# A graph network's attention passes: the sums in hand multiplied on ScalarE instead of VectorE

## The reference

```python
xl = (x @ Wl).reshape(n, H, C)
xr = (x @ Wr).reshape(n, H, C)
e = jax.nn.leaky_relu(xl[src] + xr[dst], NEG_SLOPE)
score = jnp.einsum('ehc,hc->eh', e, att)
smax = jax.ops.segment_max(score, dst, num_segments=n)
ex = jnp.exp(score - smax[dst])
denom = jax.ops.segment_sum(ex, dst, num_segments=n)
alpha = ex / jnp.maximum(denom[dst], 1e-16)
out = jax.ops.segment_sum(alpha[:, :, None] * xl[src], dst, num_segments=n)
```

## Time and profile before

| | us |
|---|---|
| median of 3 runs | 2442.35 |
| lowest, highest | 2435.42, 2443.87 |
| the profiled execution | 2437.04 |
| its span, first to last instruction | 2435.2 |

### The profile page before, as it was taken

One profiled execution on the slowest core, in us unless ns is written; L12 is line 12 of the kernel. 1 busy time (PEld: TensorE's weight loads), 2 busy tenths in 40 slices (PEclk: granted clock), 3 DMA queues, 4 the chain that ended last, 5 costly groups with the idle time before them and its releaser, 6 DMA issues. The chain is left out here.

```text
span 2435.2 us, 38029 instructions
## 1 busy us (share of the span) xinstructions
PE 1901.7 (78%) x8650; PEld 1361.5 (56%) x8650; DVE 1752.1 (72%) x3972; ACT 1347.5 (55%) x5197; POOL 1466.3 (60%) x1630
## 2 busy tenths in 40 slices
PE   4655566665569998689999999976789999999976
PEld 4443444444357775356666666653456666666654
DVE  8544333333346668589999999978489999999976
ACT  2255545555400004358777878744368788778733
POOL 3277777777700005777777677726777776767712
PEclk9777878778789999899999999998899999999987
DMA  3297676775668883355555555540355555555542
GB/s 105 65 193 173 172 163 170 177 168 167 145 206 267 269 266 112 94 158 158 154 149 166 149 151 152 147 99 30 89 158 157 158 154 151 150 154 151 142 106 83
DMA packets 225447, 370.18 MB, mean 152 GB/s; under 512 B 40453, under 2 KB 168711, under 8 KB 225256
## 3 DMA queue, kind: packets, MB, share of 16 engines
q1 hardware_dynamic: 157169, 192.55, 30.1%
q0 software_dynamic: 64512, 171.82, 25.8%
q10 hardware_dynamic: 3574, 3.66, 0.5%
HBM read 272.85 MB, written 101.50 MB: 154 GB/s over the span
## 5 line engine op out<-in xcount | busy, mean ns | idle before, releaser
L1166 POOL DMA_INDIRECT gath<-gather_table,SRCI x880 | 835.7, 950 | 321.3 <-issue 260.6
L1387 ACT ACTIVATE gath<-gath 128x32 f32<-128x32 f32 x3264 | 710.8, 306 | 0.0
L1218 PE MATMUL p_sums<-gath,OH 128*128 128x272 f32 x1760 | 474.2, 410 | 99.9 <-DVE gath L1113 60.9
L768 POOL DMA_INDIRECT rows_by_src<-gath,node x440 | 433.9, 986 | 139.6 <-issue 116.7
L702 PE MATMUL p_expd<-node,HOTS 128*128 x880 | 295.3, 496 | 228.9 <-DVE HOTS L661 220.8
L1218 PEld LDWEIGHTS p_sums<-gath,OH 128*128 128x128 f32 x1760 | 318.7, 193 | 213.9 <-issue 139.0
L702 PEld LDWEIGHTS p_expd<-node,HOTS 128*128 128x128 f32 x880 | 208.5, 248 | 304.7 <-issue 268.9
L1188 PE MATMUL p_expd<-node,LBC 128*128 x2640 | 328.9, 275 | 0.0
L1188 PEld LDWEIGHTS p_expd<-node,LBC 128*128 128x128 bf16 x2640 | 260.9, 99 | 60.3 <-issue 1.9
L1260 DVE TENSOR_REDUCE scores<-work 128x32 f32<-128x1056 f32 x220 | 274.6, 1248 | 5.7
L1182 PE MATMUL p_expd<-gath,ident 128*128 128x512 f32 x440 | 236.7, 620 | 42.8 <-DMA gath<-gather_table,SRCI 40.9
(11 more groups left out here) (291 smaller groups left out, 2767.3 us busy)
## 6 DMA issues: line engine op xcount, KB each, us to landing
gath<-rows_by_src SPq DMA_DIRECT2D x122, 514.0 KB
LBC<-hots_by_node SPq DMA_DIRECT2D x220, 128.0 KB
HOTS<-hots_by_edge SPq DMA_DIRECT2D x220, 128.0 KB, 2.6
LBC<-local_rows SPq DMA_DIRECT2D x110, 128.0 KB
hots_by_node<-gath SPq DMA_DIRECT2D x110, 128.0 KB, 5.7
hots_by_edge<-gath SPq DMA_DIRECT2D x110, 128.0 KB, 4.2
gath<-gather_table,SRCI POOLq DMA_INDIRECT x880, 3.0
rows_by_src<-gath,node POOLq DMA_INDIRECT x440, 4.9
```

What stands on the lines that cost most here:

```text
L768: pool.indirect_dma_start(sup_d[:, :], bass.IndirectOffsetOnAxis(POSI[:, i:i + 1], 0), U[:, q % 4, g, :], None, bounds_check=EP - 1, oob_i ...
L1166: pool.indirect_dma_start(ROWS[:, i % (RING * G), 0:XW], None, tab_d[:, :], bass.IndirectOffsetOnAxis(SRCI[:, i:i + 1], 0)).then_inc(gathe ...
L1218: ins = pe.matmul(sums[k][:, 0:RW], OH[:, a % 2, g, :], slots(a, g, g + 1)[:, 0, :], start=(g % 2 == 0), stop=(g % 2 == 1))
L1387: ins = act.activation(R[:, h * C:(h + 1) * C], R[:, h * C:(h + 1) * C], ACT.Copy, scale=R[:, D + h:D + h + 1])
```

## The change

ScalarE multiplies the 256 features of the sums in hand: a new function `regrow` does one operation for each head, with the head's factor as the scale. It stands behind the weighing of group 4u (`weigh_own`) and ahead of ScalarE's `ends` of the same step. VectorE keeps the 8 exponentials. A new semaphore, `regrown`, holds VectorE's next addition until the eight operations are done, and holds the next factor until the factor before it has been used.

```diff
@@ add_sum, VectorE
                             if a or k:
                                 dve.wait_ge(added, 2 * a + k)
+                            if a and a % WG == 0 and k == 0:
+                                dve.wait_ge(regrown, a // WG)
                             dve.tensor_tensor(ACC[:, bass.ds(j, 1), :], ACC[:, bass.ds(j, 1), :], sums[k][:, 0:RW].unsqueeze(1), ALU.add).then_inc(added, 1)
@@ grow, VectorE
-                            R = ACC[:, bass.ds(tile, 1), 0:D].rearrange("p a (h c) -> p (a h) c", h=H)
                             S = ACC[:, bass.ds(tile, 1), D:XW].rearrange("p a h -> p (a h)")
                             dve.wait_ge(grown, u + 1)
                             dve.wait_ge(added, 2 * WG * u)
-                            dve.tensor_tensor(R, R, GROW[:, :].unsqueeze(2).broadcast_to([P, H, C]), ALU.mult)
                             link(dve.tensor_tensor(S, S, GROW[:, :], ALU.mult))
@@ ScalarE
+                        def regrow(u):
+                            tile = tiles_of(act, 2 * WG * u, 1)[0]
+                            act.wait_ge(added, 2 * WG * u)
+                            act.wait_ge(grown, u + 1)
+                            for h in range(H):
+                                R = ACC[:, bass.ds(tile, 1), h * C:(h + 1) * C].rearrange("p a c -> p (a c)")
+                                ins = act.activation(R, R, ACT.Copy, scale=GROW[:, h:h + 1])
+                            ins.then_inc(regrown, 1)
@@ factor, ScalarE
                             act.wait_ge(risen, u + 1)
+                            if u >= 2:
+                                act.wait_ge(regrown, u - 1)
@@ ScalarE's loop over the steps
                                 if a < END_OF_ROWS:
                                     weigh_own(a)
+                            for a in batch:
+                                if a and a % WG == 0:
+                                    regrow(a // WG)
```

## The result

| | median us | lowest to highest |
|---|---|---|
| before (4 runs) | 2438.89 | 2434.12 to 2443.87 |
| changed (4 runs) | 2507.16 | 2501.82 to 2514.61 |

The ratio is 1.0273, with a 95% interval of 1.0249 to 1.0297: the change costs 68 us. The changed kernel's profiled execution took 2501.8 us, its span is 2500.0 us.

A forecast was written before the change was run, and what follows sets the result against it. VectorE was taken to bound each chunk from L1266 on, the chain ScalarE, TensorE, VectorE ahead of it. 50 x 1.28 = 64 us plus 3.6 us at pass ends, on 2442.35 us, gave 2510 us, range 2487 to 2555.

The forecast's parts named there:

- Removal worth 0: Taking L1311 (0.34 us) off VectorE gains nothing; its idle before L1247 grows from 0.32 to 0.66 us.
- R = 1.75 us: ScalarE's insertion per chunk: eight operations 1.70 us, one address step 0.05 us, register load hidden.
- rival 1: Register load and address steps show on ScalarE, or operations don't overlap: 2541 to 2602 us; chance 0.15.
- Cover 0.47 us: Sums of group 4u+1 on TensorE can take 0.47 us of ScalarE's delay before starting later.
- delay 1.28 us: Sums of group 4u+1, the turning and L1266 come 1.28 us later (1.75 - 0.47); each chunk grows by that.
- Who hands it on: ScalarE's later weighing delays TensorE's sums of 4u+1, the turning right behind them, then VectorE's L1266, by 1.28 us.
- 50 chunks and the ends of the passes: Delay counted for u = 1 to 25 in each layer, 64 us; growths 26 and 27 add 3.6 us in all.
- two waits of the sums: Sign expected in the changed profile: two waits of TensorE's sums for ScalarE per chunk, the new one about 1.3 us.
- from L1266 on VectorE alone sets the pace: From scan L1266 to the next growth VectorE has no idle but 0.21 us before that growth, so it absorbs no delay.

The follow-up runs named there:

- two heads: Changed kernel with two heads of the eight multiplied on ScalarE and six on VectorE: 2439.88 us, 0.9998 of the kernel before.
- four: Changed kernel with four heads multiplied on ScalarE and four on VectorE: 2464.28 us, 1.0094 of the kernel before.
- the turning alone: Kernel before with TensorE's turning of the scores (L1230) put ahead of the sums of its step: 2436.43 us, ratio 0.9975.
- both moves: Kernel before with ScalarE's copies L1373 and L1379 ahead of the exponentials and TensorE's turning of the scores ahead of the sums: 2423.35 us, ratio 0.9923.

## Why the prediction was right, point by point

The forecast was 2510 us (2487 to 2555), the time is 2507.2; 67.6 us were expected, 68.3 came.

- **Removal worth 0:** shown by the kernel without the multiplication (0.9995), and by the wait before L1247, 0.63 us where 0.66 were expected.
- **R = 1.75 us:** it was 0.05 us too much. The eight take 1.70 us from start to start (1310.54 to 1312.24). The register load took 0.28 us on ScalarE and the address steps 46 ns each; neither shows as a gap:

```profile
L1407 ACTq FUSED_REGOPS  x432: 46/46/52, 1082.6 to 2428.0; - x144
L1407 ACT ACTIVATE node<-node,grow x432: 304/306/322, 1082.8 to 2428.8; - x144
```

  So the 0.05 us that I let one address step show was not needed, and rival 1 (the loads and steps show) is out, with its 0.15. The load ran ahead of the weighing that stands before it:

```profile
L95 ACTq TENSOR_LOAD <-JP x1: 278/278/278, 1308.1 to 1308.1; - x1
```

  The Trainium skill (Advanced Engine Details and Errata, Engine Queue Depths) gives ScalarE's queue as 8 deep. That the load is hidden agrees with it, the number does not: the load began 0.95 us into a weighing of 16 operations that start 0.212 us apart, when 11 of them had not started.
- **Cover 0.47 us, delay 1.28 us:** the chunk grew by 22.79 - 21.51 = 1.28 us. The 0.47 us is the knee between two heads (0.04 us) and four (0.44 us, expected 0.43). That the 1.28 us came out to the hundredth is partly luck. The sums of 4u+1 are 1.21 us late, which is 1.70 us less a cover of 0.49; and from their start to the turning it takes 1.91 us (1316.56 to 1318.47) and not 1.83. The prediction left out these 0.08 us, and its 0.05 us too much in R made up for most of them.
- **Who hands it on:** TensorE's order, sums and then the turning; shown by the run in which the turnings stand ahead. ScalarE's idle before L1392 fell to 2.34 us, expected 2.3.
- **50 chunks and the ends of the passes:** 50 x 1.28 = 64 us, so 68.3 - 64 = 4 us fall to the ends, where 3.6 were expected. Both additions waited longer than forecast at the end of the first pass. From the start of the last addition to that of the next it is 2.60 us in both cases, against 1.19 us before for growth 26 and 1.58 us for growth 27, so 1.4 and 1.0 us more, where 1.1 and 0.7 were expected:

```profile
1656.55 0.44 DVE L1306 TENSOR_TENSOR node<-node,p_sums 128x272 f32 x1 [1.76 <-ACT node L1407]
...
1671.24 0.44 DVE L1306 TENSOR_TENSOR node<-node,p_sums 128x272 f32 x1 [1.77 <-PE p_sums L1218]
```

```profile
1669.20 1.81 ACT L1407 ACTIVATE node<-node,grow  x8 [3.63 <-DVE node L1306]
```

```profile
1668.98 2.07 PE L1218 MATMUL p_sums<-gath,OH 128*128 128x272 f32 x8 [1.55 <-DVE gath L1113]
```

  The profile puts the second wait down to TensorE, but the times say ScalarE. The eight end at 1671.01 and the addition starts 0.23 us later, as it does behind growth 26 (0.24 us behind 1654.51 + 1.80). It needs only the first of the group's two sums, and the next group's first addition starts 1.30 us behind the start of its sums (1672.53 to 1673.83); here it is 2.26 us. What I had too small are the gaps between engines: 0.12 us from the last addition's end to the eight, where I had none, and 0.24 us from the eight to the next addition, where I had 0.04. The first pass gave a part back behind growth 26: from the last addition ahead of it to the first instruction behind the pass it takes 20.77 us before (1623.73 to 1644.50) and 22.30 now (1653.95 to 1676.25), in the second pass 21.69 (2346.87 to 2368.56) and 24.15 (2410.59 to 2434.74), so 1.5 and 2.5 us, 4.0 together.

- **One sign was told wrongly:** I looked for two waits of the sums that the profile puts down to ScalarE in a chunk. It shows one, and the new one under issue, with 1.05 us of idle time where I looked for 1.3.
- **The statement that from L1266 on VectorE alone sets the pace** held for a delay, not for a gain: when L1266 came earlier, L1275 waited for TensorE (0.26 and 0.41 us). The prediction did not need it in that direction; my later expectations for the turning alone and for both moves did, and were 8 and 11 us too hopeful.

## What to carry to other kernels

An operation's price is set by its place in the chain and not by the busy share of its engine: 0.34 us on the busiest engine was worth nothing here, and 1.70 us on an engine with 4 us to spare in a chunk cost 1.28. For an insertion, look for the first instruction of another engine that stands behind it and had no idle time ahead of it, read off how long it was covered, and count only what goes beyond. When an engine with a fixed order hands a delay on, it can be cheaper to move the short instruction that others wait for ahead of the late one than to take the work away.

## What the runs showed of the hardware

**A VectorE operation is stretched beside GpSimd.** VectorE's multiplication of 8 exponentials, which reads and writes only the on-chip memory, took 0.17 us in the changed kernel. Beside GpSimd's multiplication of the features it takes 0.73 us, 0.56 us more, and GpSimd's own takes 0.63 us:

```profile
1310.73 0.73 DVE L1325 TENSOR_TENSOR node<-node,grow 128x8 f32 x1 [0.23 <-DVE node L1319]
```

```profile
1310.80 0.63 POOL L1176 TENSOR_TENSOR node<-node,grow 128x256 f32 x1
```

Its median over 54 is 0.728 us, so 54 x 0.56 = 30 us are in this. In the kernel with the growth wholly on GpSimd, two larger operations of VectorE fall beside it. One has an input in PSUM and kept its length (0.41 us at 1279.66); one that has both inputs in the memory was stretched from 0.41 to 0.52 us, and GpSimd's small operation beside it took 0.40 us, where it takes 0.20 us with VectorE idle (at 1617.17):

```profile
1279.99 0.52 DVE L1269 SCALAR_TENSOR_TENSOR work<-work,VEC 128x256 f32<-128x256 f32 x1
```

```profile
1279.59 0.62 POOL L1176 TENSOR_TENSOR node<-node,grow 128x256 f32 x1
1280.16 0.40 POOL L1178 TENSOR_TENSOR node<-node,grow 128x8 f32 x1
```

The Trainium skill (SBUF — State Buffer, Who interferes with whom) has it that a VectorE instruction with two inputs in the memory and a GpSimd instruction that reads it contend for a shared pair of ports, and that whoever issues first has the pair for its whole instruction. Which operations are stretched agrees. The order is not shown: in the profile VectorE's small operation starts 0.07 us ahead of GpSimd's, and it is the one that is stretched.

**TensorE's clock after idle time.** In the kernel with the eight one place later, TensorE idles 2.4 us ahead of the sums of group 4u+1. In 16 of the 18 chunks from 1132.31 to 1569.80 us its granted clock is 1.00 all the same; in two it is 0.93, and TensorE is slower behind the wait. One of the two, whole and in two stretches (start and end, length, busy us of TensorE's products, its weight loads, VectorE, ScalarE, GpSimd, then the clock, DMA share, GB/s), and the products in order of time:

```profile
1276.82:1302.61 25.79, 21.48 (x105) 14.96 (x105) 20.22 (x45) 19.05 (x85) 16.17 (x17) 0.93 0.48 129
```

```profile
1286.00:1289.00 3.00, 0.83 (x8) 0.49 (x6) 1.09 (x3) 3.00 (x14) 2.15 (x3) 1.00 0.51 152
1289.00:1292.00 3.00, 2.77 (x10) 2.15 (x11) 1.89 (x5) 2.71 (x13) 0.69 (x1) 0.75 0.53 134
```

```profile
1289.23 2.71 PE L1218 MATMUL p_sums<-gath,OH 128*128 128x272 f32 x8 [2.40 <-DVE gath L1113]
1291.73 0.42 PE L1230 MATMUL p_turned<-ident,scores 128*128 128x128 f32 x1
```

The same eight products take 2.07 us elsewhere, and the turning 0.27 us where it takes 0.42 us here. A granted clock of 0.75 is a mix of the two levels, 1.2 and 2.4 GHz, within the stretch. It fell behind 2.40 us of idle time, but the chunk after it had 2.37 us at the same place (ahead of 1315.00) and kept 1.00, so idle time alone doesn't say in which chunk it falls; what else decides is open. In the changed kernel, with 1.05 us of idle, all 19 chunks from 1146.12 to 1579.09 us have a clock of 1.00. So a delay in TensorE's chain can cost more than its own length; in the steady chunks of the changed kernel it did not.
